# A gated cross-attention and FP4 feed-forward kernel: the score shift's second operand filled by seven small DMAs instead of a TensorE product and a masked multiply

## The reference

```python
q  = layernorm(x) @ Wq      # 16 heads of 64
k, v = ctx @ Wk, ctx @ Wv
scores = q k^T / 8          # [16 heads, 100, 1444]
attn = softmax(scores)      # over the 1444
x = x + tanh(g_xattn) * ((attn @ v) @ Wo + bo)
x = x + tanh(g_ffn) * ffn(layernorm(x))     # silu-gated, 352 wide
# ffn's inputs and weights are quantised to FP4 in blocks of 16 first
```

## Time and profile before

| | |
|---|---|
| median of 3 runs | 548.21 us (547.03 to 548.56) |
| the profiled execution's own time | 547.66 us |
| its span, first to last instruction | 545.8 us |
| PE busy | 532.4 us (98% of the span) |
| DVE busy | 439.2 us (80%) |
| ACT busy | 312.8 us (57%) |
| POOL busy | 279.9 us (51%) |
| PE's granted clock | 1.00 |

### The profile page before, as it was taken

The page is one execution under the profiler, slowest core; times in us unless marked ns, Lnnn a source line. Parts: engine busy times, 40 slices in busy tenths (PEclk is TensorE's granted clock), DMA queues, the critical chain, the costliest instruction groups (busy, mean ns, idle before and its releaser), DMA issues.

```text
span 545.8 us, 8243 instructions
## 1 busy us (share of the span) xinstructions
PE 532.4 (98%) x2769; PEld 319.8 (59%) x2769; DVE 439.2 (80%) x765; ACT 312.8 (57%) x724; POOL 279.9 (51%) x260
## 2 busy tenths in 40 slices
PE   7989999999999999999999999999999999999997
PEld 4655656656565665656566565756556565655553
DVE  5868889798887979798887978789786988877865
ACT  4365546765467556765467645665567654555611
POOL 4046294745629463574927465383826566184300
PEclk9999999999999999999999999999999999999999
DMA  7502001110012100020011100120000200000000
GB/s 186 114 1 56 0 1 31 29 27 2 1 34 37 19 1 28 9 55 0 2 29 35 28 0 2 36 54 1 1 28 4 29 1 1 5 0 1 2 4 4
DMA packets 10017, 12.28 MB, mean 23 GB/s; under 512 B 4144, under 2 KB 7736, under 8 KB 9976
## 3 DMA queue, kind: packets, MB, share of 16 engines
q1 hardware_dynamic: 9000, 8.85, 6.6%
q0 software_dynamic: 560, 2.59, 3.2%
q10 hardware_dynamic: 416, 0.33, 0.2%
HBM read 11.35 MB, written 0.41 MB: 22 GB/s over the span
## 4 chain that ended last, share of the span: by engine, by line
PE 91%; DVE 6%; issue 2%; ACT 1%; POOL 0%; DVEq 0%; ACTq 0%; POOLq 0%
PE attn L931 28%; PE scores L914 19%; PE ring L840 13%; PE scores L915 12%; PE ring L857 5%; PE ring L850 4%; PE ring L820 3%; DVE max L1071 2%; PE ring L863 2%; PE ring L871 1%; PE ring L843 1%; PE attn L887 1%; ACT q_hh L638 1%; DVE e_gate L1025 0%; PE ring L799 0%
## 5 line engine op out<-in xcount | busy, mean ns | idle before, releaser
L749 ACT ACTIVATE probs<-scores 120x400 f32<-120x400 f32 (+1 forms) x384 | 185.5, 505 | 158.5 <-PE scores L915 156.1
L1071 DVE TENSOR_REDUCE max<-ring 116x1 f32<-116x482 f32 (+2 forms) x336 | 203.5, 651 | 58.2 <-PE ring L840 56.7
L592 POOL TENSOR_TENSOR acc_p<-acc_p,probs 120x800 f32<-120x800 f32 x75 | 145.2, 1936 | 64.2 <-ACT probs L749 59.9
L931 PE MATMUL attn<-probs,ctx_n 120*64 120x400 f32 (+1 forms) x768 | 170.2, 524 | 0.6 <-ACT probs L749 0.6
L914 PE MATMUL scores<-q_hh,k_hl 128*120 128x400 f32 (+1 forms) x384 | 154.6, 402 | 1.2 <-DVE q_ls L1075 0.7
L914 PEld LDWEIGHTS scores<-q_hh,k_hl 128*120 128x120 f32 (+1 forms) x384 | 69.6, 181 | 125.1 <-ACT probs L749 89.5
L915 PE MATMUL scores<-q_ls,k_h 71*120 71x400 f32 (+1 forms) x384 | 133.0, 346 | 0.0
L840 PE MATMUL ring<-k_hl,q_hh 128*116 128x482 f32 (+2 forms) x336 | 111.9, 403 | 1.9 <-DVE q_ls L1053 0.7
L915 PEld LDWEIGHTS scores<-q_ls,k_h 71*120 71x120 f32 (+1 forms) x384 | 70.3, 183 | 3.8
L931 PEld LDWEIGHTS attn<-probs,ctx_n 120*64 120x64 f32 (+1 forms) x768 | 38.3, 134 | 53.6 <-issue 33.5
L840 PEld LDWEIGHTS ring<-k_hl,q_hh 128*116 128x116 f32 (+1 forms) x336 | 58.3, 178 | 12.1 <-DVE max L1071 3.0
(11 more groups left out here) (130 smaller groups left out, 473.4 us busy)
## 6 DMA issues: line engine op xcount, KB each, us to landing
ctx_n<-in_ctx SPq DMA_DIRECT2D x8, 360.0 KB
ctxT<-in_ctxT SPq DMA_DIRECT2D x7, 361.0 KB, 4.0
k_hl<-in_ctxT POOLq DMA_DIRECT2D x7, 361.0 KB, 5.0
wvT<-in_WvT SPq DMA_DIRECT2D x2, 256.0 KB, 4.5
wo<-in_L_xattn_Wo SPq DMA_DIRECT2D x1, 512.0 KB, 5.7
x_in<-in_x SPq DMA_DIRECT2D x8, 50.0 KB
out<-y_out SPq DMA_DIRECT2D x8, 50.0 KB
ctxT<-in_ctxT SPq DMA_DIRECT2D x2, 180.5 KB, 3.9
```

Of the source, the lines that this page charges most:

```text
L592: pool.tensor_tensor(acc_p[0:r, t.g % 2, :], left, probs[0:r, c % PROBS, :], ALU.add).then_inc(sum_p, 1)
L749: act.activation(probs[0:r, c % PROBS, k * HALF:(k + 1) * HALF], scores[0:r, slot % SCORE_BANKS, 0:HALF], ACT.Exp).then_inc(probs_full, 1)
L931: mm = pe.matmul(attn[64 * i:64 * i + C, k, 0:HALF], ctx_n[0:r, par, c, :], probs[0:r, c % PROBS, k * HALF:(k + 1) * HALF], start=(j == 0) ...
L1071: dve.tensor_reduce(max3[0:rows, tile, part:part + 1], src[0:rows, 0:MAXC[part + 1] - MAXC[part]], AX.X, ALU.max).then_inc(free, 1)
```

## The change

The transposing product and the masked multiply of groups 0 to 14 are gone. Instead SP waits for max_done and issues seven DMAs, one for each tile: 116 values of 4 bytes, one from each partition of a column of maxes, into 464 contiguous bytes of one row of q_ls. Nothing writes the zeros in the other columns again: they stay from the start (a memset for one half of q_ls, the first masked multiplies for the other). The sign moves from the mask to the weights (-1.0). The second score matmul of slot 0 waits for the first four tiles, that of slot 1 for all seven, and the next group's max_tiles waits for them too. With this, the tables are written anew: pieces on all engines move by some slots.

```diff
+            def shift_rows(t):
+                half = (t.g + 1) % 2
+                if t.g == 0:
+                    sp.wait_ge(consts_set, 10)
+                sp.wait_ge(max_done, t.count(1, 3))
+                for tile in range(TILES):
+                    rows = TSIZE[tile]
+                    cols = slice(tile * TROWS, tile * TROWS + rows)
+                    sp.dma_start(q_ls[C + tile:C + tile + 1, half, cols].bitcast(F32), maxes[0:rows, tile:tile + 1].bitcast(F32)).then_inc(shift_in[tile // EARLY_TILES], 16)
...
-                if t.g % 2 == 0 and t.g >= 4 or t.g == GROUPS - 1:
+                if t.g % 2 == 0 and t.g >= 4:
+                    store(t)
+                if t.g + 1 < GROUPS:
+                    shift_rows(t)
+                else:
                     store(t)
...
                 pe.matmul(dst, k_hl[par][:, a:a + r], q_hh[:, half, cols], start=True, stop=False)
+                if t.g >= 1 and slot < 2:
+                    for part in range(k + 1):
+                        pe.wait_ge(shift_in[part], shift_count(t, part))
                 pe.matmul(dst, k_h1[par][0:C + TILES, a:a + r], q_ls[0:C + TILES, half, cols], start=False, stop=True).then_inc(scores_full, 1)
...
             def max_tiles(t, first, last, kind="max"):
                 wait_reads(dve, *[(t, (kind, 3 * last - i)) for i in (2, 1)])
+                if t.g >= 1:
+                    for k in range(2):
+                        dve.wait_ge(shift_in[k], shift_count(t, k))
...
-    if pre and slot == shift_slot:
-        keys += [("shift", 0)]
...
-PV_SLOTS = [4, 6, 8, 11, 12, 14, 16, 18, 21, 22, 24, 26]
+PV_SLOTS = [4, 4, 9, 11, 12, 14, 16, 18, 21, 22, 24, 26]
-XT_SLOT = 18
+XT_SLOT = 19
-KLO_AT = 7
+KLO_AT = 9
```

More of the change, by code:

```diff
@@ L50 @@
 SCORE_BANKS, RING_BANKS = 2, 4
-SUM_V = [0, 3, 9, 10, 11]
+SUM_V = [0, 3, 8, 10, 11]
 SUM_P = [c for c in range(CHUNKS) if c not in SUM_V]
@@ L115, in ring_keys @@
     pre = g + 1 < GROUPS
-    maxima, shift_slot = (MAX_SLOTS[g % 2], SHIFT_SLOT[g % 2]) if g else (FIRST_MAX_SLOTS, FIRST_SHIFT_SLOT)
+    maxima = MAX_SLOTS[g % 2] if g else FIRST_MAX_SLOTS
     if g == 0:
@@ L330, in xattn_ffn @@
         max_done = sem("max_done")
+        shift_in = [sem(f"shift_in{k}") for k in range(2)]
         scores_full = sem("scores_full")
@@ L565, in _ @@
             pool.wait_ge(consts_set, 6)
-            pool.affine_select(out=shift_mask[:, :, :], in_=shift_mask[:, :, :], compare_op=ALU.not_equal, fill=-1.0,
+            pool.affine_select(out=shift_mask[:, :, :], in_=shift_mask[:, :, :], compare_op=ALU.not_equal, fill=1.0,
                                base=-C, pattern=[[-1, TILES], [0, TROWS]], channel_multiplier=1).then_inc(consts_set, 1)
@@ L841, in ring_use @@
                 elif kind in ("shift", "late"):
-                    pe.wait_ge(max_done, t.count(1, 3) if kind == "shift" and t.g >= 0 else t.count(1, 2))
-                    mm = pe.matmul(dst[C:C + TILES, 0:TROWS], maxes[0:TROWS, :], ident[0:TROWS, 0:TROWS], start=True, stop=True)
+                    pe.wait_ge(max_done, t.count(1, 2))
+                    mm = pe.matmul(dst[C:C + TILES, 0:TROWS], maxes[0:TROWS, :].bitcast(F32), ident[0:TROWS, 0:TROWS], start=True, stop=True)
                 elif kind == "sum":
@@ L904, in score_slot @@
                 if slot == 0:
-                    wait_reads(pe, *[(t.before(), key) for key in (("q", 0), ("shift", 0))])
+                    wait_reads(pe, (t.before(), ("q", 0)))
                     if t.g == 0:
+                        wait_reads(pe, (t.before(), ("shift", 0)))
                         pe.wait_ge(consts_set, 9)
@@ L1072, in ring_use @@
                 elif kind == "shift":
-                    first, last = (0, TILES) if t.g >= 0 else (EARLY_TILES, TILES) if key[0] == "late" else (0, EARLY_TILES)
+                    first, last = (EARLY_TILES, TILES) if key[0] == "late" else (0, EARLY_TILES)
                     n, cols = last - first, slice(first * TROWS, last * TROWS)
-                    dve.tensor_tensor(q_ls[C:C + TILES, (t.g + 1) % 2, cols].rearrange("p (k n) -> p k n", k=n), shift_mask[C:C + TILES, first:last, :],
+                    dve.tensor_tensor(q_ls[C:C + TILES, 0, cols].rearrange("p (k n) -> p k n", k=n), shift_mask[C:C + TILES, first:last, :],
                                       src[C:C + TILES, 0:TROWS].rearrange("p (o n) -> p o n", o=1).to_broadcast([TILES, n, TROWS]), ALU.mult).then_inc(free, 1)
```

48 lines of the change are left out of this document (25 added, 23 removed).

## The result

| | before | after |
|---|---|---|
| median | 548.21 us (547.03 to 553.85, 5 runs) | 567.35 us (564.24 to 568.16, 5 runs) |
| ratio | | 1.0327, interval 1.0289 to 1.0366 |
| the profiled execution's own time | 547.66 us | 564.24 us |
| its span | 545.8 us | 562.4 us |

The ratio compares all runs of both kernels, so it isn't exactly the quotient of the medians. The forecast was 544.9 us, and 567.35 lies far above its range. The page of the kernel after answers to the earlier trace rows: first engines and their busy time, then the granted clock in 40 slices, then a group with its idle time and what ended that.

The account below looks back on a forecast made before the run. It took TensorE, busy 98% of the span, as the bound. The terms -4.6 - 0.5 - 0.1 + 0.5 + 0.7 + 0.7 = -3.3 us took the median from 548.21 to 544.9 us, range 541.8 to 551.

Parts of the forecast that it names:

- part 5: DMA arrival for slots 0 and 1: at 0.43 us an issue 1.4 and 2.2 us early, TensorE doesn't wait.
- part 6: Additions: waits of second matmuls +0.5 us; in odd groups, maximum product's bank +0.7 and later k_hl load +0.7.
- Part 1: Shift product at slots 19 to 21: hidden under ScalarE's round trip, worth nothing except -0.48 us in group 0.
- Part 2: Second PV piece moved from slot 6 to 4 in groups 1 to 14: 0.33 us each, -4.6 us.
- Part 3: Transpose of x in even groups 0 to 12, moved from slot 18 into slots 19 and 20: -0.5 us.
- Part 4: Group 0, slot 18, seven maximum products instead of five: +0.4 us; group 0 comes out at -0.1.
- (c): Seven DMAs late at slots 0 and 1 of groups 1 to 15, through slow issue or landing: 551 to 571; chance 0.12.
- (e): Packets set the DMAs' pace: four engines, 28 ns each, tiles 0.1 and 0.3 us late, 549 us; chance 0.05.
- (b): The k_hl load becomes the wait in seven odd groups: +4.9 us instead of +0.7, 549 us; chance 0.08.
- (a): Gain given back: joined PV pieces save only 0.14 us or turn into waits, no change, 548 us; chance 0.15.
- (d): Shift product does cost its 0.29 us a group: 4 us more gain, 541 us; chance 0.05.

Follow-up runs that it names:

- experiment 10: Changed kernel with KLO_AT = 6, the k_hl load behind the second layernorm's rows, plus an unused plain 361 KB load at chunk 9 of even groups: 567.7 us, ratio 1.0385.
- experiment 1: Changed kernel with KLO_AT = 6 instead of 9, so the accumulating k_hl load is issued earlier: 545.48 us, ratio 0.9941 to the kernel before.
- experiment 6: Changed kernel with unused products in the DMA wait of odd groups from 3 on: 581.08 us with six, 559.55 us with two.
- experiment 5: Changed kernel without the seven DMAs and the waits for them, tables kept: 540.77 us, ratio 0.9861 to the kernel before.
- experiment 4: Kernel before with its own tables, shift product and masked multiply left out of groups 0 to 14: 544.42 us, ratio 0.9932.
- experiment 7: Kernel before with only the second PV piece moved from slot 6 to slot 4: 544.2 us, ratio 0.9939.
- experiment 2: Changed kernel with KLO_AT = 10 instead of 9, the accumulating k_hl load one GpSimd add later: 569.74 us, ratio 1.0371 to the kernel before.

## Why the prediction was wrong

**The step that failed is part 5**, "do the DMAs arrive in time": it put TensorE's wait at nothing, and the seven DMAs cost 24.7 us of span. It priced the seven DMAs by themselves, and the load of k_hl appeared only in part 6, as something that they might delay. The delay runs the other way. The load lands after 5.0 us as before (median 5.0), and the small ones that slot 0 needs land 2 to 3 us later than they do without it. Both rows were at hand: KLO_AT = 9 put the load right behind max_tiles of the even groups. What I did not ask is what a queue of 4-byte packets gets while another queue has 5776-byte ones on the same engines. Worked out afterwards: each large packet occupies an engine for 1.015 x 16 x 2.5 / 63 = 0.64 us (101.5% of 16 engines for 2.5 us, 63 packets), 64 of them over 16 engines are four each, and beside them each of the four engines with small packets passed three. The Trainium skill (DMA: Bandwidth & Descriptors, section "Queues, rings and completion order") says that an engine serves the queue rows it has work for in turn, one packet of a row before it switches. The windows of the accumulating load agree: 12 small packets to 63 large ones, on a quarter of the engines. Those of the plain load do not: one for one would be 53 / 4 = 13 small packets, and 3 passed (experiment 10). That the small ones are held up is shown; at what rate they are let through is not settled, and on which engine a packet ran the trace does not list. The section's typical size of a packet, 9 to 17 descriptors, is not what the trace shows here: one value of 4 bytes at a time.

The numbers of part 5, one by one. The issue takes 0.67 to 0.73 us on average where no load is beside it, not 0.43: neither of the two bounds that the prediction had. From issue to release is longer too: at the start of group 15, whose maxima travel beside no load, the seventh issue starts at 510.09, and the second matmul of slot 1 is released at 512.33, after a wait of 0.18.

```profile
510.09 0.79 SPq L501 DMA_DIRECT2D q_ls<-maxes  x1
512.33 0.42 PE L937 MATMUL scores<-q_ls,k_h 71*121 71x400 f32 x1 [0.18 <-DMA q_ls<-maxes]
```

So 2.2 us, not 1.5. Of the margins of 1.4 and 2.2 us only some tenths were left: for group 6 the seventh issue starts at 216.21, its tile is there at 216.21 + 2.2 = 218.4, and slot 1 wants it at 218.53.

```profile
216.28 0.34 PE L937 MATMUL scores<-q_ls,k_h 71*121 71x400 f32 x1
218.53 0.35 PE L937 MATMUL scores<-q_ls,k_h 71*121 71x400 f32 x1
```

No wait there: without the load the DMAs do arrive, and experiment 1 shows the same for odd groups. With so small a margin nearly all of a hold-up falls on TensorE. Group 1 is a case of its own. It waits for 0.7 us with the load moved away too (experiment 1). Part 5 took the distances of group 5 for all groups, but in group 0 max_tiles stands later: it starts at 50.44 in the kernel before and at 51.10 after, in both 3.3 us ahead of the next group's slot 0, where group 5's (206.60 before) is 4.4 ahead.

```profile
55.47 0.44 PE L937 MATMUL scores<-q_ls,k_h 71*121 71x400 f32 x1 [0.68 <-DMA q_ls<-maxes]
```

**What no part had: the clock.** By experiment 6, at least 7.2 of the 22.9 us are the half clock behind a wait. It did not follow every wait. The stretches of 3.8 us behind those of groups 7, 9 and 11 (2.27, 1.86 and 2.79 us) have a granted clock of 0.55, 1.00 and 0.50:

```profile
249.49:253.30 3.81, 3.81 (x14) 2.38 (x15) 0.48 (x1) 2.03 (x5) 0.00 (x0) 0.55 0.02 4
315.04:318.80 3.76, 3.76 (x23) 2.43 (x23) 0.95 (x3) 2.82 (x6) 0.00 (x0) 1.00 0.00 0
380.01:383.80 3.79, 3.79 (x13) 2.39 (x13) 0.29 (x1) 1.86 (x4) 0.00 (x0) 0.50 0.00 0
```

Group 9 lost 2.1 us against experiment 5, hardly more than its wait; group 11 lost 7.4. Groups 3 and 13 (waits of 1.51 and 2.05 us) are like 9; group 5 is like 11, where the clock stays at 0.50 for the next 3.8 us as well. The length of the wait alone does not tell which it will be. In experiment 10 the wait of group 7 is 1.98 us, with a granted clock of 0.50 in the 3.8 us behind it, and that of group 9 is 2.03, with 1.00:

```profile
248.90 0.69 PE L943 MATMUL scores<-q_ls,k_h 71*121 71x400 f32 x1 [1.98 <-DMA q_ls<-maxes]
317.48 0.44 PE L943 MATMUL scores<-q_ls,k_h 71*121 71x400 f32 x1 [2.03 <-DMA q_ls<-maxes]
```

What else decides it stays open.

**Part 1 (the product is hidden)** was right for ordinary groups, 0.76 us against 0.75 (experiment 4). It said that "only group 0 differs", and missed groups 2 and 14, where the product waited for VectorE: together with group 0 -2.8 us, not -0.48. The view of the earlier trace rows lists these waits too, in the row `PE ring L843 <- DVE maxes L1112` of experiment 4; the prediction read one other row of it, that of the weight loads, and took its 3.0 us for all that TensorE waits for VectorE's maxima.

After's slots 19 to 21 of group 5 still last a round trip, 211.65 to 212.87 = 1.22 us, with the exponential ending the wait, as in the earlier trace rows:

```profile
211.65 0.44 PE L933 MATMUL scores<-q_hh,k_hl 128*120 128x400 f32 x1
...
212.87 0.45 PE L933 MATMUL scores<-q_hh,k_hl 128*120 128x400 f32 x1 [0.22 <-ACT probs L767]
```

**Part 2 (PV pieces joined)** was right. Two pieces take 191.78 to 193.27 = 1.49 us in an ordinary group too, as in group 15 before, and alone the move gives 0.3 us a group (forecast 0.33; experiment 7).

```profile
191.78 1.56 PE L953 MATMUL attn<-probs,ctx_n 121*64 121x400 f32 x8
193.27 0.44 PE L933 MATMUL scores<-q_hh,k_hl 128*121 128x400 f32 x1
```

**Parts 3, 4 and 6** were not tested one by one, but traces show some of them. Part 3: slots 18 to 20 of group 4 last 173.63 to 176.23 = 2.60 us before and 173.81 to 176.31 = 2.50 after, 0.1 less (forecast 0.07). Part 4: group 0 is 33.11 us long, before 32.80, so 0.3 longer, where the forecast had it 0.1 shorter. Part 6: in experiment 5 line 856, the first maximum product there, starts at 302.95 in group 9, the load issued at 297.23 has landed 1.2 us earlier, and no such product waits for it. Without the DMAs the span is 8.1 us shorter; experiments 4 and 7 give 3.2 and 3.8 of it. If these gains add up, which was not shown, 1.1 are left for the rest, where the forecast had -0.5 + 0.4 + 0.7 (bank) + 0.7 (load) = +1.3. So the additions of part 6 did not come, or were made up for; which, stays open. Apart from the DMAs the forecast of -3.3 us was thus too cautious by nearly 5.

**The rivals.** (c) had place and sign right, with 551 to 571 us and a chance of 0.12, but its mechanism, the price of the issue, was not the cause: at 0.73 us (0.82 in group 4) it is below the 0.84 from which (c) was to decide, and with the same issues experiment 1 has no such waits. (c)'s other condition, a landing over 3 us after the issue, comes nearer: the fourth tile of group 4 took 5.1. But (c) named it for the last issue, and nothing in it would make that landing late. (e) had four engines, which the packets bear out (120 a tile, for 116 values four more), and the price wrong: 8.8 ns a packet, not 28. (b) is what experiment 2 shows at KLO_AT = 10; at 9 it didn't happen. (a) and (d) fell with experiments 7 and 4.

## What to carry to other kernels

Price a small DMA together with what else is in flight when it flies: list all transfers that the same change moves, and ask which of them can stand in front of which. Price a wait of TensorE with the clock that it may cost behind it: here about 7 us beside 16 of waiting. And when a change comes with new tables, test the tables alone first: here they, with the product one slot earlier, held all of the gain (540.75 us), and the DMAs that they were made for only the loss.

## What the runs showed of the hardware

- Seven DMAs of 116 values of 4 bytes, from one value a partition into one row: 0.67 to 0.73 us an issue on SyncE on average with no load beside them, 120 packets of 8.8 ns each for a DMA, 2.2 us from the last issue's start to the release of the waiting matmul.
- Beside 63 packets of another queue, nearly all of 5776 bytes, 12 packets of 4 bytes passed in 2.5 us, and 585 in the next 1.5; with a plain load 3 beside 53 in 1.5 us.
- After idle times of 2.5 and 2.8 us TensorE's granted clock was 0.50 for 3.8 us (and 0.73 and 0.50 in the next 3.8); behind ones of 1.5, 1.9 and 2.05 us it stayed full, and so it did with two unused products in the wait. In another run 1.98 us was followed by 0.50 and 2.03 us by 1.00. A wait of 1.86 us cost 2.1 us in all, one of 2.79 cost 7.4.
